# Routed expert network in a fused two-layer block: weight split beside the router, routing and slot scatters beside a shared expert on 512-token blocks

## The chip, the cores and the metric

The kernel runs on one core of a Trainium2 chip. The metric is the device time of one execution in microseconds. The engines named are TensorE (PE; its weight loads are PEld), VectorE (DVE), ScalarE (ACT), GpSimd (POOL) and SyncE (SP), which only issues transfers here.

## What is computed

The input is 16 x 256 tokens of width 256 (4096 tokens, 32 tiles of 128). Two layers follow each other, each an attention and a feed-forward part with a gated residual. The change lies in the feed-forward part of the first layer, a mixture of 8 routed experts (two per token) and one shared expert:

```python
def _mlp(x, w1, w2, w3):
    h = jax.nn.silu(x @ w1.T) * (x @ w3.T)
    return h @ w2.T
logits = xt @ gate_w.T
scores = jax.nn.softmax(logits.astype(jnp.float32), axis=-1)
biased = scores + gate_bias
_, indices = jax.lax.top_k(biased, TOPK)
weights = jnp.take_along_axis(original_scores, indices, axis=1)
...
for e in range(E):
    y = y + _mlp(xt, w1[e], w2[e], w3[e]) * combine[:, e:e + 1]
z = _mlp(xt, sw1, sw2, sw3)
return (y + z).reshape(shape)
...
x = x + jnp.tanh(g_ffn[0]) * _L0_ffn_ref(_layernorm(x, axis=-1), ...)
```

The inner width of an expert is 512.

## The kernel before

The whole program is a row of stages with a barrier between them: setup, attention of layer 0, the expert network (`moe`), attention of layer 1, and the last feed-forward part. Every fp32 product is made as three fp16 products (`three_products`): each operand is split into a high part (a ScalarE copy to fp16) and a low part (a subtraction, original minus high part).

`moe` is itself a row of stages, each a block of its own:

1. `load_split`, first on the router's weights ("wg"), then on the 27 expert matrices ("we", 512 KB each; 9 experts, three matrices each). SyncE loads into four staging buffers, ScalarE writes the high part, VectorE the low part. A buffer is loaded again when its low part is done.
2. `moe_router`, for each tile: VectorE normalises, ScalarE makes the high part, VectorE the low part (`row`, two buffers), SyncE stores the row to DRAM (`rows`, from which tokens are gathered later), TensorE transposes it and computes the 8 logits. `high` of tile t waits until the store of tile t-2 has landed, as the buffer is the same.
3. `moe_route`: some sixty small VectorE operations on all tiles at once (softmax, two picks of the best expert, counts by a TensorE product, running sums, the slot `POS` of each token, the table `ETAB` that gives the expert of each slot tile). TensorE, ScalarE and GpSimd have next to nothing to do in it.
4. `mlp_phase` with the tag "ms", the shared expert, tile by tile (128 tokens): gate and up products of 512 columns, SiLU and product, four fp32 transposes of the hidden values, split, down product of 256 columns. Beside it `slot_table` runs on GpSimd: 64 indirect transfers (32 tiles, two picks), each of which writes 128 token numbers of 4 bytes to their slots in DRAM. They go in 16 groups of 4. Before a group's index and value buffers `idx` and `val` are written again, GpSimd waits until the transfer that last read them has landed. When all have landed, SyncE reads the table back, TensorE transposes it, and VectorE writes `IDS`.
5. `mlp_phase` with the tag "me", the routed experts, on 72 slot tiles. Its gathers need `IDS`.

In the slot scatter these lines set the order:

```python
if not first:
    scattered[q].wait(pool, i, 0)
nc.gpsimd.tensor_copy(idx[q][:], POS[:, k, bass.ds(t, 1)]).then_inc(copied, 1)
nc.gpsimd.tensor_copy(val[q][:], tok[:, bass.ds(t, 1)]).then_inc(copied, 1)
```

## Time and profile before

| | us |
|---|---|
| median of 3 runs | 2516.06 (2513.68 to 2517.75) |
| profiled execution, its own time | 2506.78 |
| span of its trace | 2504.8 |
| TensorE busy in the span | 1948.7 (78%) |
| VectorE busy | 1609.6 (64%) |
| ScalarE busy | 1111.6 (44%) |
| GpSimd busy | 876.2 (35%) |

The profiled execution is one run of its own, 9.3 us below the median of the others. Times in the trace count from the start of the span. The busy share is a mean over stages with different limits; the stages of `moe` lie between 715 and 1410 us. A row's releaser, behind an arrow, is what ended the idle time before an instruction. TensorE's granted clock is given as a share of 2.4 GHz, so 0.50 is 1.2 GHz.

### The profile page before, as it was taken

The numbers are of one execution on the slowest core, as the hardware profiler recorded it, in microseconds if no ns is written. First come the engines' busy times: TensorE is split into PE (matmuls) and PEld (weight loads), VectorE is DVE, ScalarE is ACT, GpSimd is POOL, SyncE is SP. The second block draws the span as 40 slices with busy tenths as digits, with TensorE's granted clock in tenths as the row PEclk, the third lists the DMA queues.
The fourth block names the chain that finished last, engine by engine and source line by source line (L and its number), as shares of the span: only waits on it lengthen the run. The fifth ranks groups of instructions, "written<-read, shape, count | busy, mean of one in ns | idle before, by whom it ended". The sixth has DMA issues, their size and how long they took to land. (4 is left out here: it accounts for less than half of the span.)

```text
span 2504.8 us, 48924 instructions
## 1 busy us (share of the span) xinstructions
PE 1948.7 (78%) x14975; PEld 1386.5 (55%) x14984; DVE 1609.6 (64%) x3340; ACT 1111.6 (44%) x2557; POOL 876.2 (35%) x1363
## 2 busy tenths in 40 slices
PE   1798988988904597099999679898998889994275
PEld 1576676766603364066666456676666667673122
DVE  5777777877567543044444357777777777776797
ACT  1354444544434122022222146666666666673363
POOL 2000000000000243322332377777776777762004
PEclk9899999999955799599999899999999999997598
DMA  3000000000043000012221133223222232321001
GB/s 101 9 5 8 8 4 8 8 4 4 1 160 128 7 0 1 25 54 66 70 73 57 47 97 79 61 64 83 74 71 70 62 75 74 75 56 36 0 0 67
DMA packets 91507, 118.61 MB, mean 47 GB/s; under 512 B 18264, under 2 KB 60904, under 8 KB 91368
## 3 DMA queue, kind: packets, MB, share of 16 engines
q1 hardware_dynamic: 80872, 94.74, 13.8%
q0 software_dynamic: 8576, 17.87, 2.7%
q10 hardware_dynamic: 1920, 4.19, 0.5%
q8 instruction: 81, 1.33, 0.2%
q14 instruction: 58, 0.48, 0.1%
HBM read 56.92 MB, written 17.90 MB: 30 GB/s over the span
## 5 line engine op out<-in xcount | busy, mean ns | idle before, releaser
L1112 ACT ACTIVATE a_P<-a_pS,a_NM 128x256 f32<-128x256 f32 x512 | 237.2, 470 | 158.1 <-DVE a_NM L1212 157.8
L941 POOL TENSOR_SCALAR a_P<-a_P,a_RS 128x256 f32<-128x256 f32 x512 | 255.3, 499 | 113.2 <-DVE a_RS L1216 75.6
L504 PE MATMUL a_pT<-a_Q,a_K 128*128 128x256 f32 x1024 | 243.0, 383 | 8.6 <-ACT a_PT L587 8.6
L1212 DVE TENSOR_REDUCE a_NM<-a_pS 128x2 f32<-128x512 f32 x256 | 175.5, 686 | 96.6 <-PE a_pS L1027 95.0
L587 ACT ACTIVATE a_PT<-a_pT 128x512 f32<-128x512 f32 x256 | 151.2, 597 | 187.5 <-PE a_pT L504 187.1
L420 POOL TENSOR_TENSOR a_cl<-a_ctxin,a_ch 128x512 f16<-128x512 f32 x16 | 18.6, 1160 | 542.5 <-ACT a_ch L557 542.5
L504 PEld LDWEIGHTS a_pT<-a_Q,a_K 128*128 128x128 f32 x1024 | 183.6, 190 | 38.8 <-ACT a_PT L587 16.5
L1222 DVE TENSOR_TENSOR a_PL<-a_pT,a_PH 128x512 f16<-128x512 f32 x256 | 173.6, 678 | 48.2 <-ACT a_PH L1121 48.0
L1121 ACT ACTIVATE a_PH<-a_pT 128x512 f16<-128x512 f32 x256 | 153.1, 598 | 110.0 <-PE a_pT L1035 95.5
L1035 PE MATMUL a_pT<-g_ident,a_P 128*128 128x128 f32 x1024 | 157.9, 277 | 43.8 <-POOL a_P L941 34.8
L694 DVE TENSOR_REDUCE a_M<-a_pS 128x2 f32<-128x512 f32 x256 | 162.8, 682 | 32.8 <-PE a_pS L483 32.2
L1035 PEld LDWEIGHTS a_pT<-g_ident,a_P 128*128 128x128 f32 x1024 | 117.4, 141 | 74.9 <-POOL a_P L941 52.4
L1027 PE MATMUL a_pS<-a_KZ,a_QS 128*128 128x256 f16 x512 | 125.9, 273 | 0.0
L1026 PE MATMUL a_pS<-a_KD,a_QS 128*128 128x256 f16 x512 | 125.8, 273 | 0.0
L1707 ACT ACTIVATE me_hh<-me_pH 128x512 f16<-128x512 f32 x72 | 43.0, 597 | 175.7 <-PE me_pH L1692 175.7
L99 PE MATMUL a_pF<-a_ch,xw_XW 128*128 128x256 f16 x512 | 98.3, 276 | 27.2 <-DVE a_VL L1205 23.1
L1756 DVE TENSOR_TENSOR me_h<-me_SG,me_pU 128x512 f32<-128x512 f32 x72 | 49.5, 687 | 98.5 <-PE me_pU L99 98.5
L1705 ACT ACTIVATE me_SG<-me_pG 128x512 f32<-128x512 f32 x72 | 43.0, 597 | 147.8 <-PE me_pG L99 147.8
L99 PE MATMUL me_pG<-mo_w1h,me_xt 128*128 x288 | 98.7, 384 | 6.9 <-issue 6.9
L1112 ACT ACTIVATION_READ_ACCUMULATOR a_P<-a_pS,a_NM 128x1 f32 x512 | 102.8, 201 | 0.0
L99 PE MATMUL a_pF<-a_xh,xw_XW 128*128 128x256 f16 x512 | 98.9, 273 | 2.4 <-DVE a_k L1198 2.4
L1023 PE MATMUL a_pS<-a_maskq,g_identb 128*128 128x512 bf16 x256 | 97.4, 380 | 2.9 <-POOL a_maskq L931 2.4
(410 smaller groups left out, 5507.5 us busy)
## 6 DMA issues: line engine op xcount, KB each, us to landing
a_KD<-a_KN SPq DMA_DIRECT2D x128, 128.0 KB
a_QS<-a_QN SPq DMA_DIRECT2D x128, 128.0 KB
we_stage<-mw SPq DMA_DIRECT2D x24, 512.0 KB, 4.7
ys<-me_yb SPq DMA_DIRECT2D x72, 128.0 KB, 1.7
a_ctxin<-ctxT SPq DMA_DIRECT2D x32, 256.0 KB, 2.8
a_KZ<-a_KN SPq DMA_DIRECT2D x64, 128.0 KB
g_X<-x SPq DMA_DIRECT2D x1, 4096.0 KB, 15.0
rows<-mr_row SPq DMA_DIRECT2D x32, 128.0 KB, 1.7
```

Of the source, the lines that this page charges most:

```text
L99: last = nc.tensor.matmul(out, a(kt), b(kt), start=(n == 0), stop=(n == 3 * chunks - 1))
L504: last = nc.tensor.matmul(pT[h % 2][:, kt, :], K32[par][h % 2][:, h // 2, kt * P:(kt + 1) * P], Q32[par][:, h // 2, :], start=True, stop=True)
L587: nc.scalar.activation(PT[h % 8][:], pT[h % 2][:], ACT.Exp, scale=float(dh) ** -0.5).then_inc(p_ready.sem, 1)
L694: nc.vector.reduce_max(M[:, k % 2, k - k % 2:k - k % 2 + 2], pS[k % 2][:], AX.X).then_inc(s_max.sem, 1)
L941: last = nc.gpsimd.tensor_scalar(P32[u % 4][:, a, :], P32[u % 4][:, a, :], RS[u % 4][:, a:a + 1], LIFT, ALU.mult, ALU.mult)
L1026: nc.tensor.matmul(out[:, a, :], q, KD2[par][a][:, p2, :], start=False, stop=False)
L1027: last = nc.tensor.matmul(out[:, a, :], q, KZ[par][a][:, p2, :], start=False, stop=(a == 1))
L1035: last = nc.tensor.transpose(pT[u % 2][:, a, kt, :], P32[u % 4][:, a, kt * P:(kt + 1) * P], ident[:])
L1112: last = nc.scalar.activation(P32[u % 4][:, a, :], pS[u % 2][:, a, :], ACT.Exp, bias=NM[u % 4][:, a:a + 1], accum_out=SM[u % 4][:, a:a + 1])
L1121: nc.scalar.activation(PH[p2 % 2][:, :, :, j * P:(j + 1) * P].rearrange("p a k q -> p (a k) q"), pT[u % 2][:].rearrange("p a k q -> p (a k ...
L1212: nc.vector.tensor_reduce(NM[u % 4][:], pS[u % 2][:], AX.X, ALU.max, negate=True).then_inc(s_max.sem, 1)
L1222: nc.vector.tensor_tensor(PL[p2 % 2][:, :, :, j * P:(j + 1) * P].rearrange(f), pT[u % 2][:].rearrange(f), PH[p2 % 2][:, :, :, j * P:(j + 1 ...
```

## The change

- `load_split` for the router's and the experts' weights goes. The 27 loads, high parts and low parts move into the block of `moe_router`: SyncE issues the loads, ScalarE makes the high parts (`weight_high`, one a tile), GpSimd the low parts. The row stores move from SyncE to ScalarE. Loops are unrolled.
- `moe_route`, `slot_table` and the shared expert's `mlp_phase` become one block, `moe_shared`. The shared expert works on 8 blocks of 512 tokens. Its weights are the stationary operand of gate and up, so the hidden values come out transposed and the four transposes a tile go. One step g (32 in all) makes 128 of the 512 hidden rows for 512 tokens. Behind gate and up of steps 4, 8, ... stand the four down products of the block before (`down`), and those of the last block stand at the end. Gate and up have two PSUM buffers each; `h`, `SG`, `hh` and `hl` have one.
- The routing operations are put behind VectorE's `hidden` of steps 0 to 9 (`routing`). The slots are final in step 7 (`placed`).
- The 64 scatters read `POS` and `tok` directly and are issued one after the other, with one wait by SyncE at their end.
- The rotary tables are freed behind attention 0; that moves addresses only.

```diff
-def moe_router(nc, ctx, X, mean, rstd, XT, gwh, gwl, rows_d, L, consts):
+def moe_router(nc, ctx, X, mean, rstd, XT, gw_d, rows_d, L, consts, jobs):
     s = Scope(nc, ctx, "mr")
+    NS = 4
...
+    stage = [s.sb(f"stage{i}", [P, KD * F0]) for i in range(NS)]
...
+            sp.dma_start(gin[:], gw_d.rearrange("(k p) n -> p k n", p=P)).then_inc(gate_in, 16)
+            for j, (src, hi, lo) in enumerate(jobs):
+                if j >= NS:
+                    sp.wait_ge(w_lo, j - NS + 1)
+                sp.dma_start(stage[j % NS][:].rearrange("p (a b) -> p a b", a=src.shape[1]), src).then_inc(staged[j % NS], 16)
+        @block.gpsimd
+        def _(pool):
+            for j, (src, hi, lo) in enumerate(jobs):
+                pool.wait_ge(w_hi, j + 1)
+                nc.gpsimd.tensor_tensor(lo, stage[j % NS][:], hi, ALU.subtract).then_inc(w_lo, 1)
...
+            dve.wait_ge(gate_hi, 1)
+            nc.vector.tensor_tensor(gwl[:], gin[:], gwh[:], ALU.subtract).then_inc(gate_lo, 1)
...
+            def high(t):
                 xn_ready.wait(act, t, 1)
-                if pair is not None:
-                    stored[q].wait(act, pair, 0)
+                if t > 1:
+                    stored[t % 2].wait(act, t // 2, 0)
                     xt_full.wait(act, t, -1)
-                nc.scalar.activation(row[q][:, 0, :], xn[q][:], ACT.Copy).then_inc(hi_ready.sem, 1)
-            def logits(t, q):
+                nc.scalar.activation(row[t % 2][:, 0, :], xn[t % 2][:], ACT.Copy).then_inc(hi_ready.sem, 1)
+            def store(t):
+                lo_ready.wait(act, t, 1)
+                nc.scalar.dma_start(rows[t, :, :], row[t % 2][:].rearrange("p a d -> p (a d)")).then_inc(stored[t % 2].sem, 16)
+            def logits(t):
                 l_full.wait(act, t, 1)
-                nc.scalar.activation(L[:, bass.ds(t, 1), :].rearrange("p a e -> p (a e)"), pL[q][:], ACT.Copy).then_inc(l_out.sem, 1)
-            high(0, 0, None)
-            high(1, 1, None)
-            with act.Fori(0, TILES // 2 - 1) as i:
-                for q in range(2):
-                    high(i * 2 + 2 + q, q, i + 1)
-                    logits(i * 2 + q, q)
-            logits(TILES - 2, 0)
-            logits(TILES - 1, 1)
+                nc.scalar.activation(L[:, t, :], pL[t % 2][:], ACT.Copy).then_inc(l_out.sem, 1)
+            def weight_high(j):
+                src, hi, lo = jobs[j]
+                act.wait_ge(staged[j % NS], 16 * (j // NS + 1))
+                nc.scalar.activation(hi, stage[j % NS][:], ACT.Copy).then_inc(w_hi, 1)
+            high(0)
+            high(1)
+            for t in range(TILES):
+                store(t)
+                if t < len(jobs):
+                    weight_high(t)
+                if t + 2 < TILES:
+                    high(t + 2)
+                logits(t)
...
+def moe_shared(nc, ctx, X, XT, W1, W3, W2, consts, gb_d, slots_d, L, POS, GW, ETAB, IDS):
+    ident, gates = consts[0], consts[7]
+    s = Scope(nc, ctx, "ms")
     TE = [P, TILES, NE]
+    BLOCKS, BT = TILES // 4, 4 * P
+    STEPS = BLOCKS * FK
+    SG, h = s.sb("SG", [P, BT]), s.sb("h", [P, BT])
...
+    scan = (bi, cand)
...
+            sp.wait_ge(zero_ready, 1)
+            by_slot = slots_d.rearrange("(s p) a -> s (p a)", p=P)
+            sp.dma_start(by_slot, table[:]).then_inc(zeroed, 16)
+            sp.wait_ge(scattered, 16 * TOPK * TILES)
+            sp.dma_start(table[:], by_slot).then_inc(table_in, 16)
...
+            pool.wait_ge(zeroed, 16)
+            pool.wait_ge(placed, 1)
+            nc.gpsimd.nop(nofuse=True)
+            for t in range(TILES):
+                for k in range(TOPK):
+                    nc.gpsimd.indirect_dma_start(out=slots_d, out_offset=bass.IndirectOffsetOnAxis(ap=POS[:, k, t:t + 1], axis=0),
+                                                 in_=tok[:, t:t + 1], in_offset=None).then_inc(scattered, 16)
...
+            def up(g):
+                n, m = g // FK, g % FK
+                ts, fs = slice(n * BT, (n + 1) * BT), slice(m * P, (m + 1) * P)
+                for bank, W, full, free in ((pG, W1, gate_full, silu_ready), (pU, W3, up_full, h_ready)):
+                    if g > 1:
+                        free.wait(pe, g, -1)
+                    three_products(nc, bank[g % 2][:], lambda kt: W[0][:, NE, kt, fs], lambda kt: W[1][:, NE, kt, fs],
+                                   lambda kt: XT[:, 0, kt, ts], lambda kt: XT[:, 1, kt, ts], KD).then_inc(full.sem, 1)
+            def down(t):
+                j = t % 4
+                hl_ready.wait(pe, (t // 4 + 1) * FK, 0)
+                if t > 1:
+                    y_out.wait(pe, t, -1)
+                js = slice(j * P, (j + 1) * P)
+                three_products(nc, pY[t % 2][:], lambda k: hh[:, k, js], lambda k: hl[:, k, js],
+                               lambda k: W2[0][:, NE, k, :], lambda k: W2[1][:, NE, k, :], FK).then_inc(y_full.sem, 1)
+            for g in range(STEPS):
+                up(g)
+                if g == COUNT_AT:
+                    pe.wait_ge(counts_in, 1)
+                    nc.tensor.matmul(pC[:, 0:256], earlier[:], picked[:].rearrange("p t e -> p (t e)"), start=True, stop=True)
+                    nc.tensor.matmul(pC[:, 256:512], ones[:], picked[:].rearrange("p t e -> p (t e)"), start=True, stop=True)\
+                        .then_inc(counted, 1)
+                if g % FK == 0 and g:
+                    for t in range(g - 4, g):
+                        down(t)
+            for t in range(TILES - 4, TILES):
+                down(t)
+            pe.wait_ge(table_in, 16)
+            nc.tensor.transpose(pI[:], table[:], ident[0:SLOT_TILES, 0:SLOT_TILES]).then_inc(ids_full, 1)
...
+            def silu(g):
+                gate_full.wait(act, g, 1)
+                if g:
+                    h_ready.wait(act, g, 0)
+                nc.scalar.activation(SG[:], pG[g % 2][:], ACT.Silu).then_inc(silu_ready.sem, 1)
+            def high(g):
+                n, m = g // FK, g % FK
+                h_ready.wait(act, g, 1)
+                if n:
+                    y_full.wait(act, 4 * n, 0)
+                nc.scalar.activation(hh[:, m, :], h[:], ACT.Copy).then_inc(hh_ready.sem, 1)
+            for g in range(STEPS):
+                silu(g)
+                high(g)
...
+            def routing(g):
+                if g == 0:
+                    softmax_out()
+                    choose(0)
+                elif g == 1:
+                    choose(1)
+                elif g == COUNT_AT:
+                    counts()
+                elif g == COUNT_AT + 1:
+                    running(0)
+                elif g == COUNT_AT + 2:
+                    running(1)
+                elif g == COUNT_AT + 3:
+                    expert_starts()
+                elif g == COUNT_AT + 4:
+                    positions()
+                elif g == COUNT_AT + 6:
+                    expert_table()
+            def hidden(g):
+                up_full.wait(dve, g, 1)
+                silu_ready.wait(dve, g, 1)
+                if g:
+                    hh_ready.wait(dve, g, 0)
+                    hl_ready.wait(dve, g, 0)
+                V.tensor_tensor(h[:], SG[:], pU[g % 2][:], ALU.mult).then_inc(h_ready.sem, 1)
+            def low(g):
+                n, m = g // FK, g % FK
+                hh_ready.wait(dve, g, 1)
+                if n:
+                    y_full.wait(dve, 4 * n, 0)
+                V.tensor_tensor(hl[:, m, :], h[:], hh[:, m, :], ALU.subtract).then_inc(hl_ready.sem, 1)
+            def result(t):
+                y_full.wait(dve, t, 1)
+                V.scalar_tensor_tensor(X[:, t, :], pY[t % 2][:], gates[:, 2:3], X[:, t, :], ALU.mult, ALU.add).then_inc(y_out.sem, 1)
+            softmax_in()
+            for g in range(STEPS):
+                hidden(g)
+                routing(g)
+                if g >= FK and g % FK == 0:
+                    for t in range(g - 4, g):
+                        result(t)
+                low(g)
+            for t in range(TILES - 4, TILES):
+                result(t)
+            y_out.wait(dve, TILES, 0)
+            dve.wait_ge(ids_full, 1)
+            V.tensor_copy(IDS[:], pI[:])
...
+    jobs = [(w_d[n][e].rearrange("(k p) n -> p k n", p=P), W[n][0][:, e, :, :].rearrange(flat), W[n][1][:, e, :, :].rearrange(flat))
+            for e in (NE, *range(NE)) for n in ("w1", "w3", "w2")]
...
-        load_split(nc, c2, "wg", [(gw_d.rearrange("(k p) n -> p k n", p=P), gw[0][:].rearrange(flat), gw[1][:].rearrange(flat))], KD * NE)
+        moe_router(nc, c2, X, mean, rstd, XT, gw_d, rows_d, L, consts, jobs)
     with ExitStack() as c2:
-        jobs = [(w_d[n][e].rearrange("(k p) n -> p k n", p=P), W[n][0][:, e, :, :].rearrange(flat), W[n][1][:, e, :, :].rearrange(flat))
-                for n in ("w1", "w3", "w2") for e in range(NE + 1)]
-        load_split(nc, c2, "we", jobs, KD * F0)
+        moe_shared(nc, c2, X, XT, W["w1"], W["w3"], W["w2"], consts, gb_d, slots_d, L, POS, GW, ETAB, IDS)
     with ExitStack() as c2:
-        moe_router(nc, c2, X, mean, rstd, XT, gw[0], gw[1], rows_d, L, consts)
-    with ExitStack() as c2:
-        moe_route(nc, c2, L, gb_d, consts[7], consts, tok, POS, GW, ETAB)
-    with ExitStack() as c2:
-        table = slot_table(nc, c2, slots_d, tok, POS, IDS, consts[0])
-        mlp_phase(nc, c2, "ms", TILES, X, XT, W["w1"], W["w3"], W["w2"], consts, None, table)
-    with ExitStack() as c2:
-        mlp_phase(nc, c2, "me", SLOT_TILES, X, XT, W["w1"], W["w3"], W["w2"], consts, (IDS, ETAB, rows_d, y_d), None, (XW, next_w_d))
+        mlp_phase(nc, c2, "me", SLOT_TILES, W["w1"], W["w3"], W["w2"], consts, (IDS, ETAB, rows_d, y_d), (XW, next_w_d))
```

ScalarE in the router's block. `mr_row` is the row's high part, `mo_L` the logits, `mo_w1h` and the like are high parts of expert weights. Before, the split and then the router's loop body:

```order
L273 ACTIVATE mo_w1h<-we_stage 128x1024 x9
L273 ACTIVATE mo_w3h<-we_stage 128x1024 x9
L273 ACTIVATE mo_w2h<-we_stage 128x1024 x9
L260 UNCONDITIONAL_BRANCH
L1303 UNCONDITIONAL_BRANCH
L1310 ACTIVATE mr_row<-mr_xn 128x256 x2
```

Now, from the start of the router's block:

```order
L1320 ACTIVATE mr_row<-mr_xn 128x256 x2
L1324 DMA rows<-mr_row 128x512
L1333 ACTIVATE mo_w1h<-mr_stage 128x1024
L1320 ACTIVATE mr_row<-mr_xn 128x256
L1328 ACTIVATE mo_L<-mr_pL 128x8
L1324 DMA rows<-mr_row 128x512
L1333 ACTIVATE mo_w3h<-mr_stage 128x1024
```

The row store and one weight's high part now stand between two rows' high parts, in ScalarE's own queue.

GpSimd at the slot scatter (`slots` is the table in DRAM). Before, one group of the loop:

```order
L1522 COPY st_idx<-g_POS 128x1
L1523 COPY st_val<-mo_tok 128x1
L1522 ISA
L1522 COPY st_idx<-g_POS 128x1
L1523 COPY st_val<-mo_tok 128x1
L1524 ISA
L1527 DMA slots<-st_val,st_idx 9216x1 x4
```

Now:

```order
L1431 MEMSET ms_earlier 128x128
L1432 MEMSET ms_ones 128x128
L1434 AFFINE_SELECT ms_earlier<-ms_earlier 128x128
L1437 MEMSET ms_table 72x128
L1443 DMA slots<-ms_tok,g_POS 9216x1 x64
```

The copies, and with them the waits for landed transfers, are gone, and all 64 transfers stand in a row.

VectorE in step 7 of the shared expert's block, now (`ms_h` is the hidden product, `ms_hl` its low part; before, the routing rows stood in a block of their own, ahead of all `ms_h` rows):

```order
L1618 TENSOR_TENSOR ms_h<-ms_SG,ms_pU 128x512
L1575 TENSOR_TENSOR ms_excl<-ms_excl,ms_bi 128x256
L1576 TENSOR_TENSOR ms_excl<-ms_excl,ms_tot 128x256
L1577 TENSOR_TENSOR ms_excl<-ms_excl,ms_first 128x256
L1579 TENSOR_TENSOR ms_tmp<-ms_oh,ms_excl 128x256
L1580 TENSOR_REDUCE ms_posf<-ms_tmp 128x32
L1579 TENSOR_TENSOR ms_tmp<-ms_oh,ms_excl 128x256
L1580 TENSOR_REDUCE ms_posf<-ms_tmp 128x32
L1581 CAST g_POS<-ms_posf 128x64
L1625 TENSOR_TENSOR ms_hl<-ms_h,ms_hh 128x512
```

The slots are ready only when VectorE has passed seven steps of the shared expert.

## Rows read from the trace of the kernel before

**Rows 1.** Windows by stage: busy time and count per engine, PEclk, DMA share, GB/s
```profile
717.50:769.50 52.00, 0.00 (x0) 0.00 (x0) 33.07 (x27) 28.52 (x27) 0.00 (x0) 0.50 0.82 272
769.50:818.30 48.80, 30.07 (x320) 25.00 (x320) 34.90 (x96) 17.90 (x64) 0.00 (x0) 0.50 0.26 86
818.30:845.30 27.00, 0.61 (x2) 0.13 (x2) 20.83 (x63) 1.70 (x2) 1.62 (x7) 0.50 0.00 0
845.30:990.00 144.70, 141.42 (x896) 89.33 (x896) 59.57 (x96) 39.49 (x65) 60.15 (x145) 0.98 0.01 1
990.00:1055.00 65.00, 0.38 (x1) 0.18 (x1) 0.23 (x1) 0.00 (x0) 20.79 (x49) 0.52 0.01 1
```

**Rows 2.** Timeline, 1038 to 1060 us: start, length, engine, line, operation
```profile
1041.44 0.95 POOL L1527 DMA_INDIRECT slots<-st_val,st_idx  x1 [0.30 <-issue]
1042.70 0.96 POOL L1527 DMA_INDIRECT slots<-st_val,st_idx  x1 [0.31 <-issue]
1049.77 0.30 SPq L1509 DMA_DIRECT2D st_back<-slots  x1
...
1055.37 0.18 POOL L1609 COPY me_idx<-mo_IDS 128x1 uint32<-128x1 uint32 x1 [11.71 <-POOLq L1600]
```

**Rows 3.** Timeline of SyncE, 715 to 819 us
```profile
715.15 0.38 SPq L266 DMA_DIRECT2D wg_stage<-gate_w  x1
...
818.40 0.34 SPq L1387 DMA_DIRECT2D rt_gb<-gate_bias  x1
```

**Rows 4.** Page, part 6: DMA issues, size, median us to landing
```profile
we_stage<-mw SPq DMA_DIRECT2D x24, 512.0 KB, 4.7
...
rows<-mr_row SPq DMA_DIRECT2D x32, 128.0 KB, 1.7
```

**Rows 5.** Groups of instructions, 700 to 1056 us, with mean ns of one
```profile
L1760 DVE TENSOR_TENSOR ms_hl<-ms_pH,ms_hh 128x512 f16<-128x512 f32 x32 | 22.1, 691 | 15.9 <-ACT ms_hh L1707 15.7
L1756 DVE TENSOR_TENSOR ms_h<-ms_SG,ms_pU 128x512 f32<-128x512 f32 x32 | 22.0, 687 | 45.5 <-PE ms_pU L99 44.3 <-issue 1.3
...
L1707 ACT ACTIVATE ms_hh<-ms_pH 128x512 f16<-128x512 f32 x32 | 19.1, 597 | 78.2 <-PE ms_pH L1692 78.2
L1705 ACT ACTIVATE ms_SG<-ms_pG 128x512 f32<-128x512 f32 x32 | 19.1, 597 | 23.6 <-PE ms_pG L99 23.6
...
L1310 ACT ACTIVATE mr_row<-mr_xn 128x256 f16<-128x256 f32 x32 | 13.2, 416 | 21.9 <-DMA rows<-mr_row 17.3 <-DVE mr_xn L1278 4.6
...
L273 ACT ACTIVATE mo_w1h<-we_stage 128x1024 f16<-128x1024 f32 x9 | 9.5, 1056 | 9.3 <-DMA we_stage<-mw 9.1 <-DMA we_stage<-msw 0.3
```

**Rows 6.** Tile me_stage: duration ns min/median/max of the GpSimd subtraction
```profile
L1606 POOL TENSOR_TENSOR xw_XW<-me_stage,xw_XW x8: 2124/2126/2132, 1109.1 to 1373.1; 128x1024 f16<-128x1024 f32 x8
```

**Rows 7.** Timeline of TensorE, one tile of the shared expert
```profile
903.65 0.38 PE L99 MATMUL ms_pG<-mo_w1h,xw_XW 128*128 128x512 f16 x1
...
906.24 0.27 PE L99 MATMUL ms_pY<-mo_w2h,ms_hh 128*128 128x256 f16 x1
...
907.55 0.60 PE L1692 MATMUL ms_pH<-g_ident,ms_h 128*128 128x128 f32 x4
```

**Rows 8.** Timeline of VectorE: the slot positions
```profile
842.74 0.19 DVE L1482 CAST g_POS<-rt_posf 128x64 uint32<-128x64 f32 x1
```

**Rows 9.** Timeline of GpSimd, index copies of three of the groups
```profile
860.43 0.18 POOL L1522 COPY st_idx<-g_POS 128x1 uint32 x1 [5.80 <-DMA slots<-st_val,st_idx]
...
865.30 0.18 POOL L1522 COPY st_idx<-g_POS 128x1 uint32 x1
...
1008.89 0.18 POOL L1522 COPY st_idx<-g_POS 128x1 uint32 x1 [1.88 <-DMA slots<-st_val,st_idx]
...
1017.12 0.18 POOL L1522 COPY st_idx<-g_POS 128x1 uint32 x1 [1.95 <-DMA slots<-st_val,st_idx]
...
1033.85 0.18 POOL L1522 COPY st_idx<-g_POS 128x1 uint32 x1 [0.90 <-DMA slots<-st_val,st_idx]
...
1037.83 0.18 POOL L1522 COPY st_idx<-g_POS 128x1 uint32 x1 [2.17 <-DMA slots<-st_val,st_idx]
```

323 lines of the change are left out of this document (133 added, 190 removed).

## The prediction

> **What bounds the kernel now.** I read the busy time by stage first, then the timeline where the stages meet, then the groups inside each. The expert network is a row of stages with a barrier between, so a microsecond saved in one is a microsecond saved in the whole as long as its slowest chain is what gets shorter. Four stages lie before the routed experts [rows 1]. The weight split (717.5 to 769.5) keeps the transfer engines 0.82 busy at 272 GB/s and TensorE idle. The router (769.5 to 818.3) moves 86 GB/s; its ScalarE waits for landed row stores (17.3 us of waits behind 13.2 us of work, [rows 5]). The routing (818.3 to 845.3) is VectorE alone. The shared expert fills TensorE until 990 (141.4 of 144.7 us), but the routed experts cannot start then: from 990 to 1055 TensorE has one product, and only GpSimd works. The last slot scatter is issued at 1042.70, its landing releases SyncE's read of the table at 1049.77, and the next stage starts at 1055.37 [rows 2]. So the scatters, not TensorE, end the shared expert's stage. From the first load at 715.15 [rows 3] to 1055.4 it is 340 us. The routed experts behind are not touched, and I carry them over unchanged.
>
> **Router and split in one block.** Removed is the split's own time, 52 us, with the router weights' block of 2.4 us ahead of it. What is added to the router is, for each of 27 tiles, a high part of 1.06 us on ScalarE [rows 5], a subtraction on GpSimd, which takes 2.13 us for the same shape in the routed stage [rows 6], and a 512 KB load. The sums by engine are all below the 100.8 us that the two stages take: GpSimd 27 x 2.13 = 57 us; ScalarE 27 x (1.06 + 0.42 + 0.15, the logits copy from 17.9 - 13.2 us over 32) = 44 us and 32 issues.
>
> The chain is what counts. ScalarE now issues the store of tile t, makes a weight's high part, and then waits until that same store has landed, since the next row's high part of tile t+2 goes to the same buffer. Before, SyncE issued the stores, and two were under way together. Now ScalarE cannot issue store t+1 until store t has landed. A tile takes at least 1.7 us to landing [rows 4] + 0.42 + 0.15 + about 0.2 for hand-overs = 2.45 us; the weight's high part is hidden in the landing. Beside it 655 KB move per tile, which at 272 GB/s is 2.4 us: the transfer engines are nearly as tight, so a store shares them with a load. The landing grows with the queue (a load lands after 4.7 us where several are under way, [rows 4]). I take 0.3 us more, 2.75 us a tile. The bounds are 2.45 and 3.3 us (a GpSimd subtraction of 2.13 and the two VectorE operations of 0.42 in turn, plus hand-overs). The stage: 4 us for the router weights, 27 x 2.75, 5 x 2.45 for the tiles without weights, 3 us for the end = 93.5 us, against 103.2 now. The gain is 10 us (from 18 less to 5 more time), far below the 52 us of the stage removed. The block ends at 808.6.
>
> The Trainium skill (SBUF — State Buffer, the part on the shared port pair) says that a GpSimd operation and a VectorE operation with two SBUF inputs lock each other out for a whole instruction; by it the upper bound of 3.3 us a tile would be the value. No row before has the two side by side in this form.
>
> **The shared expert and the routing.** Now a tile costs TensorE 2.59 us for gate and up (903.65 to 906.24), 1.31 us for down (to 907.55) and the transposes behind [rows 7]. The transposes go; 32 steps of 2.59 and 32 downs of 1.31 are 125 us. The routing's 24.6 us (818.3 until the slots' cast ends at 842.93, [rows 1, 8]) now lies between the shared expert's own operations on VectorE. Up to step 7 these add 8 hidden products and 7 low parts of 0.69 [rows 5] = 10.4 us, four results (2 us), and one wait for four down products (5.2 us) with hand-overs to ScalarE's 0.6 us copies: about 6 us. The slots are ready 43 us into the block, not 24.6. TensorE starves meanwhile: `h` has one buffer, and gate and up may run only two steps ahead. Step 7's low part releases the downs of block 1, done at about 50 us; that includes 1 us for a start at 1.2 GHz (clock 0.50 in the stages before, 0.98 in this one, [rows 1]). Behind it stand 23 x 2.59 + 24 x 1.31 = 91 us, then 4 us for the last block's SiLU, product, copy and subtraction in a row before the last downs: 145 us, and 2.5 us to the next stage. In the steady part VectorE needs 4 x 1.38 + 2 = 7.5 us a block of four tiles and TensorE 15.6, so nothing else waits.
>
> **The scatters** decide. Two things are removed: 128 small copies and the wait for landing between groups. GpSimd's issue takes 1.26 us apiece (1041.44 to 1042.70, [rows 2]): 64 are 81 us. But are landings as fast as issues? Within a group the four are issued 1.26 us apart, and the copies for the second and the fourth, each released by the landing of the transfer before, should stand 2.5 us apart. They stand 4.87 us apart in the loop's first group, 3.98 in its last, 8.23 in the slowest [rows 9]; over all 15 groups of the loop the mean is 4.11 us. So four scatters under way land every 2.06 us. This is a rate, not only a delay: if each had the same delay, the landings would keep the distance of the issues. I take 2.06 us. Then the last lands 1 + 64 x 2.06 + 3 us behind the slots: 43 + 136 = 179 us. From the read of the table to the next stage it is 5.6 us [rows 2]. The stage takes 184.5 us and ends at 993, and TensorE has an idle gap of some 35 us in front of that, down from 65.
>
> The Trainium skill (DMA: Bandwidth & Descriptors, "Anatomy of one DMA") puts most of a transfer's fixed 2 us in the receipt of its last write, which queued transfers overlap; by it the scatters would go at the pace of issue. The spacing of the landings [rows 9] does not agree with it for these 4-byte writes. The same page's table of specifications says that transfers under 512 bytes are read-modify-writes, which speaks for the slower rate.
>
> **The sum.** The routed experts start at 993 instead of 1055.4: 62 us less. The profiled execution of 2506.8 us would be 2445; it lies 9 us below the median of the runs shown, so for a median I forecast 2516 - 62 = 2454 us.
>
> **Rivals.**
> - *Issue-paced scatters* (0.30). Landings overlap as issues do: 43 + 1 + 81 + 5 + 5.6 = 136 us, less than TensorE's 147.5, which then ends the stage, at 956. That is 99 us less: 2417. For it: the short distances (some groups have two landings released almost together). Against: the mean of 2.06.
> - *Slower landings under a deep queue* (0.17). Now the queue empties after each four; with 64 queued it never does. A whole group takes 12.3 us (865.30 to 1037.83 is 14 groups, [rows 9]), of which some 11 us are from first issue to last landing, 2.75 us apiece: 44 + 176 + 3 + 5.6 = 229 us, end at 1037, 18 us less: 2498.
> - *The landings lose more than the waits cost* (0.05; slower than before). With the rest as forecast, the start at 1055.4 is reached when each scatter takes (1055.4 - 808.6 - 52.6) / 64 = 3.03 us. At the slowest group's 8.23 / 2 = 4.1 us the stage lasts 315 us, 68 us over: 2584. For it: one group has it. Against: only one in fifteen.
> - *The router's block is slower than forecast* (0.06), 3.3 us a tile, with the scatters as in my case: 47 us less, 2469.
> - The split into two states, issue-paced or landing-paced, is the main doubt; my own case has 0.40. Its own range is 2440 to 2475 (1.8 to 2.4 us a scatter, router's block 88 to 100 us). Within 0.2% of before, about what a measurement of this kernel can tell from no change, lies only a narrow band around 3.03 us a scatter: 0.02.
>
> **Range and chances.** From the issue-paced case with the shorter router block (2417 - 8) to nearly the deep-queue case: 2405 to 2495. Faster 0.93, same 0.02, slower 0.05.
>
> **What the changed profile would show.** The router's block 88 to 100 us long, with ScalarE idle before each row's high part for the landed store, and GpSimd's subtractions near 2.13 us. VectorE's cast of the slots 43 us into the shared block. GpSimd's 64 scatters 1.26 us apart in one row of 81 us (if they stand further apart, their queue is full). SyncE's read of the table 179 us into the block; if it stands at 130 us or before TensorE's last product, the landings overlap and the first rival is right. TensorE near 2.59 us a step from step 9 on. A low clock in the first 45 us of the block, where TensorE has gaps, would move the TensorE end later, but counts only in the issue-paced case. What would make me wrong is above all the landing rate, 64 times in the sum: 0.1 us in it is 6.4 us.

## The result, and the profile after

The changed kernel took 2429.93 us (median of 4 runs, 2424.18 to 2436.15) beside 2516.9 us of the kernel before: ratio 0.9654, 95% interval 0.9626 to 0.9683. That is 24 us less than the 2454 forecast and inside the range. Timed again, in two later batches of runs (both on one chip; on which the first ran is not recorded), the same program took 2504.67 us (7 runs, 2491.85 to 2509.36) and 2501.20 us (7 runs, 2496.73 to 2509.09), both times 0.9945 of the kernel before (0.9922 to 0.9969, and 0.9927 to 0.9964). So it is faster in all three, but by 3.5% once and by 0.55% twice. The first part of this section reads the profile of the fast measurement (2431.72 us); the experiments are mostly about the difference.

Windows of the changed kernel, cut at its stages, against [rows 1]: length, busy time and count of each engine, PEclk, DMA share, GB/s.

```profile
713.30:818.40 105.10, 24.10 (x320) 21.09 (x320) 51.45 (x97) 43.69 (x92) 58.06 (x27) 0.50 0.59 175
818.40:862.30 43.90, 34.52 (x160) 16.40 (x161) 30.84 (x78) 12.67 (x20) 1.81 (x8) 0.85 0.01 2
862.30:966.00 103.70, 98.71 (x604) 60.02 (x603) 48.41 (x81) 27.56 (x47) 63.01 (x64) 0.97 0.03 2
```

The first row is the joined block of weights and router: 105 us, no shorter than the two stages that it replaces (100.8 us in [rows 1]), although it does both at once. From its first load to the load of the bias it is 106.4 us (713.36 to 819.74, below), where it was 103.2 before. The second runs until the scatters start, the third while they are issued, with TensorE busy in 98.71 of 103.7 us.

The router's rows and (last line) normalised tiles in that block, by tile: durations min/median/max, first and last start, what ended the idle time before it, and the landing of its store. Line 1324 answers to the last of [rows 4], line 1320 to the mr_row line of [rows 5].

```profile
L1320 ACT ACTIVATE mr_row<-mr_xn x32: 416/416/417, 715.8 to 815.4; 128x256 f16<-128x256 f32 x32
...
L1324 ACTq DMA_DIRECT2D rows<-mr_row x32: 326/326/392, 716.7 to 817.1; - x32
...
  DMA rows<-mr_row: 53.3, 29
...
DMA to landing us min/median/max: 1.7/3.2/5.7
...
L1290 DVE TENSOR_SCALAR mr_xn<-g_X,g_mean,g_rstd x32: 398/406/2280, 715.4 to 812.2; 128x256 f32<-128x256 f32 x32
```

Beside the weight loads a store lands after 3.2 us, up to 5.7, where it was 1.7; ScalarE sits idle for it 53.3 us. VectorE's normalisation takes 0.40 us at its shortest and 2.28 us at its longest, where a GpSimd subtraction lies beside it. The low part of a row, which reads two tiles, is held up likewise; here from 743.22 to 745.02 us, beside a subtraction that ends at 744.74:

```profile
742.51 2.23 POOL L1280 TENSOR_TENSOR mo_w3l<-mr_stage,mo_w3h 128x1024 f16<-128x1024 f32 x1 [0.69 <-ACT mo_w3h L1333]
...
743.22 1.80 DVE L1294 TENSOR_TENSOR mr_row<-mr_xn,mr_row 128x256 f16<-128x256 f32 x1 [0.46 <-ACT mr_row L1320]
```

The timeline of the shared block and what frames it: SyncE's three transfers, then VectorE's cast of the slot positions, then GpSimd's first and last scatter and the first index copy of the next stage. They answer to [rows 2, 3, 8].

```profile
713.36 0.38 SPq L1270 DMA_DIRECT2D mr_gin<-gate_w  x1
...
819.74 0.34 SPq L1418 DMA_DIRECT2D ms_gb<-gate_bias  x1
...
951.09 0.29 SPq L1423 DMA_DIRECT2D ms_table<-slots  x1
...
861.22 0.20 DVE L1581 CAST g_POS<-ms_posf 128x64 uint32<-128x64 f32 x1
...
862.30 1.23 POOL L1443 DMA_INDIRECT slots<-ms_tok,g_POS  x1 [40.99 <-DVE g_POS L1581]
...
943.56 0.95 POOL L1443 DMA_INDIRECT slots<-ms_tok,g_POS  x1 [0.30 <-issue]
968.20 0.19 POOL L1708 COPY me_idx<-mo_IDS 128x1 uint32<-128x1 uint32 x1 [23.69 <-POOLq L1415]
```

The positions of the slots are cast at 861.2, 41.5 us into the block. The 64 scatters leave from 862.30 to 943.56, 1.29 us apart. The table is read at 951.09, only 7.5 us after the last of them was issued: landings keep up with issues. TensorE's last product of the block starts at 966.85 and the routed experts' first index copy follows at 968.20, against 1055.37 in [rows 2]: 87.2 us earlier. The medians differ by 87.0 us, but the two profiled executions by 75.1 only: some of the 87.2 us is given back behind this point. The view of the gathers of the second attention (first and last start) shows most of it:

```profile
L901 POOL DMA_INDIRECT a_routed<-ys,a_pick x64: 971/1049/1084, 1331.7 to 2107.1; - x64
```

The first starts 87.1 us earlier than in the profile of before (1418.8 there) and the last 78.1 earlier (2185.2 there): 9 us lost in a stage that the diff does not touch. In the middle of the scatters TensorE is never idle for long:

```profile
880.00:940.00 60.00, 59.52 (x370) 36.11 (x371) 26.94 (x45) 16.52 (x28) 45.67 (x48) 1.00 0.03 2
```

One line in this profile looks harmless. Two rows of ScalarE's timeline, each a copy that opens a block of four tiles and so waits for TensorE's four down products of the block before:

```profile
916.81 0.63 ACT L1497 ACTIVATE ms_hh<-ms_h 128x512 f16<-128x512 f32 x1 [6.00 <-PE ms_pY L99]
...
936.62 0.63 ACT L1497 ACTIVATE ms_hh<-ms_h 128x512 f16<-128x512 f32 x1 [10.21 <-remote]
```

`remote` stands where a signal arrived but no instruction whose end fits it is in the records. The wait is 6.00 us in the two blocks before and 10.21 us here, 4.2 us more. In the two later measurements of this program the longest wait with this mark is some 31 us, and the experts start 63 to 71 us later.

### The profile page after: what moved, and what is told of

It reads as the page before. It is cut to its first block and busy times, and to the rows that moved or that the text cites. A ratio compares the mean times of both kernels' runs of the same rounds, so it can differ in the third digit from the quotient of the medians.

```text
span 2430.0 us, 47541 instructions
## 1 busy us (share of the span) xinstructions
PE 1941.7 (80%) x14847; PEld 1372.2 (56%) x14856; DVE 1592.0 (66%) x3313; ACT 1108.4 (46%) x2557; POOL 917.0 (38%) x1262
## 5 line engine op out<-in xcount | busy, mean ns | idle before, releaser
L99 PE MATMUL me_pU<-mo_w3h,me_xt 128*128 x288 | 98.3, 382 | 0.0
```

Of the source, the lines that this page charges most:

```text
L99: last = nc.tensor.matmul(out, a(kt), b(kt), start=(n == 0), stop=(n == 3 * chunks - 1))
```

## The experiments

The runs came in four batches, each on one chip with its own runs of the kernel before: 2522.62 us (19 runs) for the first four kernels, 2515.48 (10) for the next four, 2515.27 (7) for three, 2518.53 (10) for the last. The first, second and third batch ran on three different chips, the last on that of the second.

### The scatters alone

The kernel before, with its scatters freed of the copies and of the waits between groups:

```diff
-        def scatter(i, first):
...
-        scatter(0, True)
-        with pool.Fori(1, TILES * TOPK // NB) as i:
-            scatter(i, False)
+        for t in range(TILES):
+            for k in range(TOPK):
+                nc.gpsimd.indirect_dma_start(out=slots_d, out_offset=bass.IndirectOffsetOnAxis(ap=POS[:, k, t:t + 1], axis=0),
+                                             in_=tok[:, t:t + 1], in_offset=None).then_inc(all_scattered, 16)
```

> The kernel before, with only the slot scatters issued one after the other without waits (the rest is as before: split, router, routing and shared expert in their own stages). Theory A, landings overlap as issues do: the scatters end 81 + 8 us behind their start, before TensorE's last product at 990, the routed experts start at 992 instead of 1055, about 63 us less (ratio 0.975). Theory B, landings come every 2 us once several are under way: the scatters end 847 + 135 = 982 and the gain is the same; theory C, at 2.75 us: end at 1028, gain 25 us. The read of the table by SyncE tells A (near 936) from B (near 982).

Measured: 2520.62 us, 0.9992 (0.9981 to 1.0004): nothing gained. The scatters did go at the pace of issue, 850.8 to 930.6 us, and the table was read at 939.5. But the routed experts started at 1069.7, later than before. A window of 60 us in the middle of the scatters:

```profile
870.00:930.00 60.00, 7.85 (x28) 3.95 (x28) 1.86 (x3) 0.60 (x1) 45.64 (x48) 0.53 0.02 0
```

and three rows of the view of waits, 830 to 1000 us: who waited for what, us in total, times, longest:

```profile
ACT ms_hh L1691 <- remote: 51.2, 2, 45.7
...
PE ms_pY L99 <- issue: 38.1, 2, 36.2
...
DVE g_X L1728 <- remote: 31.6, 2, 28.9
```

TensorE worked 7.85 of the 60 us. So landings are not the limit that the prediction took them for; something else happens to TensorE, ScalarE and VectorE while scatters leave closely, and it eats the whole gain.

### Scatters in fours, each four landed

The changed kernel, with a wait for everything issued before each four scatters:

```diff
             for t in range(TILES):
+                if t and t % 2 == 0:
+                    pool.wait_ge(scattered, 16 * TOPK * t)
                 for k in range(TOPK):
```

> The changed kernel, with GpSimd waiting for all landings after every four scatters, as the kernel before does in effect; nothing else is changed. If the waits were the cost: a group takes about 11 us again, 16 groups 180 us, the table is read at 862 + 180 = 1042 instead of 951, and the time is 75 to 95 us above the changed kernel (2510). If the small index copies were a large part of the cost before, the groups take under 9 us and the time is less than 50 us above.

Measured: 2530.95 us, 1.0033 (1.0018 to 1.0047). GpSimd waited 115.8 us in 15 waits, the scatters lasted from 867.4 to 1059.6, and the experts started at 1071.8. TensorE was busy 59.41 of 60 us between 880 and 940, and then waited 100.8 us for the table. A group took 12.6 us, more than the 11 expected, and the read of the table stood at 1067.4, not 1042. With this wait left in, the whole change is worth nothing.

### Four row buffers in the router's block

```diff
-    xn = [s.sb(f"xn{i}", [P, D]) for i in range(2)]
-    row = [s.sb(f"row{i}", [P, 2, D], F16) for i in range(2)]
+    NR = 4
+    xn = [s.sb(f"xn{i}", [P, D]) for i in range(NR)]
+    row = [s.sb(f"row{i}", [P, 2, D], F16) for i in range(NR)]
...
-                if t > 1:
-                    stored[t % 2].wait(act, t // 2, 0)
+                if t >= NR:
+                    stored[t % NR].wait(act, t // NR, 0)
```

> The changed kernel with four buffers instead of two for the normalised rows and their fp16 parts in the router's block, so that ScalarE waits for the landing of the store of two tiles further back. Theory A, the landing of the store is the chain (53 us of ScalarE's waits): a tile takes about 2.5 us instead of 3.45, set by the loads, the block 80 to 88 us instead of 105, 17 to 25 us less (2408). Theory B, GpSimd's and VectorE's locking each other out is the chain: less than 5 us.

Measured: 2472.80 us, 0.9810 (0.9783 to 0.9837). SyncE's timeline, the frame of the block:

```profile
716.52 0.38 SPq L1271 DMA_DIRECT2D mr_gin<-gate_w  x1
...
796.26 0.34 SPq L1419 DMA_DIRECT2D ms_gb<-gate_bias  x1
```

and the view of the rows' tile, for VectorE's low part and the landing of the stores:

```profile
L1295 DVE TENSOR_TENSOR mr_row<-mr_xn,mr_row x32: 410/412/2142, 719.6 to 792.3; 128x256 f16<-128x256 f32 x32
...
DMA to landing us min/median/max: 1.7/3.8/6.0
```

From the gate's load to the bias's it is 79.7 us instead of 106.4 (713.36 to 819.74). (In the other three profiles of this block with two row buffers it is 98.0, 108.0 and 108.0 us; in all with four, 79.5 to 81.3.) The stores land no sooner (3.8 us median) and VectorE is still stretched (2142 ns at the longest), so what bounded the block was ScalarE's wait for the buffer that a store still reads. Yet the routed experts started at 1014.5, where some 945 was to be had (148.5 us behind the bias load, as in the first profile of the changed kernel). The 60 us after 860, as a window:

```profile
860.00:920.00 60.00, 11.19 (x36) 4.77 (x36) 2.83 (x4) 2.45 (x4) 45.55 (x48) 0.50 0.02 1
```

and five operations from the timeline of the same stretch, of TensorE, ScalarE, VectorE, ScalarE and TensorE:

```profile
869.14 0.63 PE L99 MATMUL ms_pU<-xw_XW,mo_w3l 128*128 128x512 f16 x1
...
880.40 0.60 ACT L1491 ACTIVATE ms_SG<-ms_pG 128x512 f32<-128x512 f32 x1 [12.75 <-issue]
...
897.20 0.69 DVE L1619 TENSOR_TENSOR ms_h<-ms_SG,ms_pU 128x512 f32<-128x512 f32 x1 [28.76 <-remote]
...
897.92 0.63 ACT L1498 ACTIVATE ms_hh<-ms_h 128x512 f16<-128x512 f32 x1 [16.92 <-issue]
...
899.33 0.40 PE L99 MATMUL ms_pY<-mo_w2h,ms_hh 128*128 128x256 f16 x1 [29.55 <-issue]
```

These rows show the stall from near. The product `h` needs TensorE's up-product, whose last matmul starts at 869.14, and ScalarE's SiLU, done at 881.0. VectorE starts it at 897.20, 16 us after the later of the two. ScalarE's copy of it follows within 0.03 us, and TensorE's next product 0.06 us behind VectorE's low part (898.58 to 899.27). So instructions on ScalarE and VectorE start at once behind each other, but those that wait for a TensorE result (`gate_full`, `up_full`, `y_full`) wait some 15 to 30 us; and since `h` and the banks have one and two buffers, everything stands. The clock falls to 0.50 as well (the lower of its two levels, 1.2 GHz), with TensorE idle for most of the window; in the windows with no stall it is 1.00.

These waits have to be read with care. The 64 scatters give 1024 landing signals (16 each). Counted up to the read of the table, the trace of the kernel before holds 1011 of them and the first profile of the changed kernel 910, but this one 164. Of the engines' own signals it holds 5 between 860 and 920 us, where the first profile has 112 between 880 and 940. So `remote` and `issue` often stand here only because the signal is missing from the records; the starts and lengths of the instructions don't depend on that.

### Router and weights apart again

The changed kernel's shared block behind the old two stages:

```diff
-def moe_router(nc, ctx, X, mean, rstd, XT, gw_d, rows_d, L, consts, jobs):
+def moe_router(nc, ctx, X, mean, rstd, XT, gwh, gwl, rows_d, L, consts):
...
+        load_split(nc, c2, "we", jobs, KD * F0)
+        moe_router(nc, c2, X, mean, rstd, XT, gw[0], gw[1], rows_d, L, consts)
```

> The changed kernel with the weight split and the router of the kernel before, each a stage of its own again; the shared expert's block as changed. Theory A, the fusion of split and router gives nothing, since ScalarE waits for each row store to land (105 us for the block against 103 us for the two stages): within 3 us of the changed kernel, rather 2 us faster. Theory B, the fusion gives something that the block's length does not show (a warmer clock later on): more than 5 us slower.

Measured: 2489.25 us, 0.9870 (0.9850 to 0.9891), 59 us above the changed kernel's first measurement. The bias was loaded at 817.72, 104.8 us behind the first load, within the 98.0 to 108.0 us of the joined block: joining gained no time that stands clear of this spread. TensorE was starved here too (10.38 of 60 us from 880 to 940), and the experts started at 1035.9. That is where the changed kernel starts them when it stalls (1031.6 and 1039.2, below), and yet it takes 2501 to 2505 us then. The gathers of the second attention, by tile:

```profile
L901 POOL DMA_INDIRECT a_routed<-ys,a_pick x64: 971/1049/1083, 1397.8 to 2167.2; - x64
```

From first to last they take 769.4 us here, 766.4 in the kernel before and 767.0 in the one with the scatters alone. In every kernel with the joined block they take 773.9 to 777.4 us. So this second attention takes 4.5 to 8 us longer behind the joined block than in this run. Its loops are also unrolled where the old stages have loops, and these runs do not show which of the two it is, or why.

At this point three of three kernels with free scatters stalled and the changed kernel had not. Either its program was spared or its measurement; the next four runs were to tell.

### The changed kernel again, beside four in flight

First a wait that keeps scatters apart, with four row buffers:

```diff
             for t in range(TILES):
+                if t > 1:
+                    pool.wait_ge(landed[t % 2], 16 * TOPK * (t // 2))
                 for k in range(TOPK):
```

> The changed kernel with four row buffers in the router block, and before each group of four scatters (from the third on) a wait until the group two before it has landed, so that at most eight are in flight. Theory Q (the run of the four row buffers lost its gain because the ungated scatters delay what the other engines wait for; eight in flight is what the kernel before had, without any such delay): TensorE is busy over 90% of the time while the scatters are issued, as it was in the kernel before, the index copy of the routed experts starts at 945 to 970 us instead of 1014.5, and the time is 2405 to 2435 us against 2522 of the kernel before (0.954 to 0.965). Theory R (the delay has nothing to do with how many are in flight, but with this chip or with where the program lies in memory): the same starvation as with ungated scatters, index copy near 1014, 2473 us (0.981).

A group here is two scatters, so at most four were in flight, not eight as the expectation says; the kernel before also had four.

> The changed kernel with four row buffers and ungated scatters once more, beside the changed kernel itself. Theory Q, and theory R by placement of the program: as before, about 2473 us with TensorE idle for most of 80 us. Theory R by chip: the same on a chip where the changed kernel itself stalls, and about 2410 us on one where it doesn't.

> The changed kernel itself, unaltered, on the chip of the other runs of this call. If the stall of the three ungated variants comes from the chip, it is here too: TensorE starved for 60 to 80 us behind the first scatter, 2485 us or so against 2522 (0.985). If it comes from the kernels and not the chip: TensorE busy over 90% as in its first profile, 0.9654 again, 2435 us.

> The changed kernel with four row buffers, ungated, but each of the 64 scatters writes only the tokens of partitions 0 to 63 (half of the slots keep token 0, so the routed experts work on wrong rows; the amount of their work is unchanged). If the delay grows with the number of 4-byte writes under way, it is halved or gone: index copy at 945 to 985 us and 2405 to 2445 us. If it comes with the number of scatter instructions or with something else, index copy near 1014 and 2473 us.

```diff
-out_offset=bass.IndirectOffsetOnAxis(ap=POS[:, k, t:t + 1], axis=0), in_=tok[:, t:t + 1]
+out_offset=bass.IndirectOffsetOnAxis(ap=POS[0:64, k, t:t + 1], axis=0), in_=tok[0:64, t:t + 1]
```

Measured: four in flight 2447.11 us, 0.9729 (0.9708 to 0.9749); the ungated four-row kernel 2476.55 (one run); the changed kernel 2504.67, 0.9945; half of the writes 2476.11 (one run). A window of 60 us beside the scatters, with four in flight:

```profile
860.00:920.00 60.00, 60.00 (x365) 35.39 (x363) 28.93 (x47) 18.99 (x32) 27.60 (x29) 1.00 0.02 1
```

of the ungated four-row kernel:

```profile
860.00:920.00 60.00, 5.52 (x24) 3.36 (x24) 2.07 (x3) 1.75 (x3) 43.34 (x46) 0.54 0.02 0
```

of the changed kernel:

```profile
880.00:940.00 60.00, 11.25 (x36) 4.82 (x36) 4.23 (x8) 3.05 (x5) 45.68 (x48) 0.51 0.02 1
```

and of the one with half of the writes, 50 us, since its scatters end sooner:

```profile
860.00:910.00 50.00, 8.22 (x18) 2.21 (x18) 5.07 (x10) 1.86 (x3) 37.41 (x42) 0.52 0.02 1
```

The changed kernel itself stalls: 11.25 of 60 us, where its first profile has 59.52. The view of its waits between 864 and 960 us, for VectorE and TensorE:

```profile
DVE ms_h L1618 <- remote: 62.5, 3, 31.5
...
PE ms_pY L99 <- issue: 29.6, 4, 24.6
PE ms_pY L99 <- DVE g_X L1629: 27.7, 1, 27.7
```

Its experts started at 1039.2, not 968.2, and that is the difference between the two measurements: 71 us later, 74.7 us more time. So the stall comes with the change itself and not only with its variants, and the first measurement is the one that was spared. In this batch four row buffers are worth 28.1 us (2504.67 less 2476.55, the latter a single run). With four in flight no stall is left, and the scatters take 838.7 to 973.8 us, 2.14 us apart; TensorE then waits 42.8 us for the table. The experts start at 985.1, later than the 945 to 970 expected of eight in flight. With half as many 4-byte writes in each scatter the stall is the same (8.22 of 50 us), so halving the writes does not ease it. It does bring the last landing forward: the table is read 2.8 us behind the last issue (916.24 less 913.42), where it is 6.8 to 9.0 us with all writes. With landings so early some two or three scatters can be in flight there, if the others land as the last does (an estimate, 2.8 us at 1.21 us apart); that is no more than in the run with at most four, which does not stall. (That kernel leaves the token of half of the slots at 0; the amount of the experts' work is unchanged.)

### Paced by time, and six in flight

The wait of the last kernel keeps fewer scatters in flight and also spreads them. Pacing without any wait for a landing:

```diff
                                                  in_=tok[:, t:t + 1], in_offset=None).then_inc(scattered, 16)
+                    for r in range(2):
+                        if t + k + r:
+                            pool.wait_ge(paused, 2 * (TOPK * t + k) + r)
+                        nc.gpsimd.memset(pause[:], 0.0).then_inc(paused, 1)
```

> The changed kernel with four row buffers and ungated scatters, but with two small GpSimd memsets behind each scatter, so that the scatters leave about every 2.1 to 2.4 us and GpSimd never waits for a landing (eight_in_flight above had in truth four in flight, since a group there is two scatters, and a pitch of 2.1 us). Theory P (what delays TensorE's signals is how densely the scatters are issued): no stall, TensorE busy over 90% until about 942 us, the last scatter at 975 to 990, the index copy at 990 to 1000, 2450 to 2462 us against 2515 to 2522 of the kernel before. Theory F (it is the wait for landings that protects): TensorE stalls as in the ungated runs, with waits put down to remote of 15 us and more, and since the scatters last longer the index copy comes after 1040, over 2495 us.

Six in flight, by the wait for the third group back:

```diff
             for t in range(TILES):
+                if t > 2:
+                    pool.wait_ge(landed[(t - 3) % 4], 16 * TOPK * ((t - 3) // 4 + 1))
                 for k in range(TOPK):
```

> As the gated run with four row buffers, but with up to six scatters in flight (groups of two, a wait for the third group before). A landing there took about four pitches, 8.4 us, so six in flight allow a pitch of 1.4 us. If the delay of the other engines grows smoothly with the density of scatters: waits of 5 to 10 us begin to show at TensorE, the index copy starts at 955 to 985 and the time is 2415 to 2445 us. If there is a threshold between a pitch of 1.4 and 1.26: no stall, index copy at 945 to 952, 2405 to 2412 us, 0.956 of the kernel before. If the threshold lies under six in flight: starved as ungated, index copy near 1014, 2473 us.

> The ungated kernel with four row buffers, as the reference of this call: on the two chips so far 2473 and 2477 us with the index copy at 1014.5 and 1011.0. About the same is expected wherever scatters at a pitch of 1.26 us starve the other engines; 2405 to 2415 us would mean a chip or a placement on which they don't, as in the first profile of the changed kernel.

Measured: paced 2454.25 us (one run); six in flight 2426.94 us (2421.34 to 2438.19), 0.9643 (0.9627 to 0.9659); ungated 2472.23 (one run). The same 60 us, paced:

```profile
860.00:920.00 60.00, 60.00 (x364) 35.40 (x363) 28.84 (x46) 18.96 (x32) 54.05 (x82) 1.00 0.02 1
```

six in flight:

```profile
860.00:920.00 60.00, 39.33 (x220) 22.40 (x218) 15.98 (x26) 9.79 (x17) 37.91 (x40) 0.89 0.03 1
```

ungated:

```profile
860.00:920.00 60.00, 10.25 (x35) 4.41 (x32) 3.44 (x5) 2.45 (x4) 45.67 (x48) 0.50 0.02 1
```

The scatters by tile (durations, first and last start), paced:

```profile
L1445 POOL DMA_INDIRECT slots<-ms_tok,g_POS x64: 963/966/1524, 837.5 to 978.5; - x64
```

and six in flight:

```profile
L1448 POOL DMA_INDIRECT slots<-ms_tok,g_POS x64: 953/960/1477, 839.9 to 946.6; - x64
```

The stall goes with the distance between scatters, with four row buffers throughout:

| kernel | distance, us | TensorE busy, of 60 us | experts start | time, us |
|---|---|---|---|---|
| paced, no wait | 2.24 | 60.00 | 988.6 | 2454.25 |
| four in flight | 2.14 | 60.00 | 985.1 | 2447.11 |
| six in flight | 1.69 | 39.33 | 976.1 | 2426.94 |
| ungated (three profiles) | 1.27 | 11.19, 5.52, 10.25 | 1014.5, 1011.0, 1013.8 | 2472.80, 2476.55, 2472.23 |

(The distance is last start less first over 63.) In the paced kernel GpSimd is busy 54.05 of 60 us and nothing stalls, so it is not GpSimd's being busy. The numbers with six in flight are those expected of a stall that grows smoothly with density. Six in flight is the best of these: it pays some stall, and the table comes before TensorE has done. Its profiled run was its slowest (2438.19 us); the other three are at 2421.34 to 2428.82.

### The changed kernel a third time

> The changed kernel itself a third time. It has been timed twice: 2429.93 us (0.9654 of the kernel before), with TensorE hardly delayed beside the scatters, and 2504.67 us (0.9945), starved for some 80 us behind them. If the first was an exception (one chip or one placement) and starvation at a pitch of 1.26 us is the rule, as in the six other profiles with ungated scatters: 2490 to 2510 us, index copy at 1030 to 1045. If it goes by chip with no rule: either of the two levels, about 2430 or about 2500, and all runs of one call at the same level. If it goes by single executions: both levels among the runs of this call.

Measured: 2501.20 us, 0.9945, all seven runs between 2496.73 and 2509.09; the experts started at 1031.6. The earlier repeat had been on this same chip, so this confirms the level but adds no chip. The levels did not mix within a batch. Eight profiles with scatters 1.21 to 1.28 us apart, on three chips and in five different programs, show the starvation; the first profile of the changed kernel is the only one without.

## Why the prediction was right, and where it was not

**The direction and the number.** Faster, with 2429.93 in the range of 2405 to 2495, came true in the first measurement. In the repeats the time lay 6 to 10 us above the range. That the first number came within 24 us is in part luck: the shared stage took 36 us less than forecast (148.5 against 184.5), the router's block 12.9 more, and 12.1 us of the profiled gain were given back behind the experts' start, where the prediction carried everything over unchanged. In the repeats a further cost was there, which no term stood for.

**Router and weights, forecast 93.5 us: mis-sized.** From first load to bias load, as the forecast counts, it measured 106.4 us, and 108.0 and 98.0 in the repeats. Only the last lies in the 88 to 100 us named; all lie below the 108.4 that 3.3 us a tile would give. The mechanism was as forecast (ScalarE idle for the landed store, 53.3 us), but a tile took (807.2 - 717.6) / 26 = 3.45 us, first to last high part of a weight, against 2.75 and even against the bound of 3.3. The failed number is "I take 0.3 us more": the store landed 1.5 us later at the median beside a load, and up to 4 us later. Four buffers took 26.6 us off, so the term was this wait and not the turns of GpSimd and VectorE. The turns are there, though: VectorE's low part, with its two SBUF inputs, stretched from 0.41 to 1.80 us beside GpSimd's subtraction of some 2.15. On this the trace agrees with the Trainium skill (SBUF — State Buffer, on the shared port pair). The normalisation, with one tile as input, stretched too, from 0.40 to 2.28 us. The bound of 3.3 us a tile, worked out from such turns, was passed since a store alone took 3.2 us to land at the median and 5.7 at most.

**Slots ready after 43 us: right** (41.5). **TensorE done after 145 us: right**, 147.2 us (819.74 to 966.96) with one small delay in it.

**The scatters, 2.06 us apiece: wrong, and this is the step that failed.** The sentence "This is a rate, not only a delay: if each had the same delay, the landings would keep the distance of the issues" was drawn from landings in groups of four with a pause behind each. Their distances (4.11 us at the mean for two issued 2.5 us apart) tell how delays differ within such a group, not how fast landings can follow each other. With all freed the table could be read 7.5 us after the last issue, in the first profile of the changed kernel, and after 6.8 to 9.0 us in the other ungated ones with all writes (951.8 less 945.0; 928.6 less 919.6). In the kernel before it was 7.1 us (1049.77 less 1042.70), paced 6.1, with four in flight 7.2, with six 7.3: about the same delay at every distance from 1.27 to 2.24 us, so a delay that overlaps and not a rate. The first rival (issue-paced, 0.30) was right: it gave 136 us to the next stage by the scatters, 147.5 by TensorE, against 148.5 measured (819.7 to 968.2). The Trainium skill (DMA: Bandwidth & Descriptors, "Anatomy of one DMA") puts most of a transfer's fixed time in the receipt of its last write; the prediction concluded from it that queued transfers overlap this time and then set that aside, and the runs bear the conclusion out for these 4-byte writes. The rival's 2417 us and the router's 12.9 us above forecast make 2429.9; 2429.93 was measured. That this fits so closely is chance, since 12.1 us behind the experts' start are in no term and the profiled run of before lies 9.3 us under its median.

**What no case had: the stall.** At a distance of 1.27 us TensorE stood for most of 80 us in eight of nine profiles. It takes back 63 to 71 us of the 87 that the change had won by the start of the experts in its first profile. The deep-queue rival (0.17) feared the right situation, a queue that never empties, but expected the landings to suffer; they did not, the other engines did. The profile of before could not show it: its scatters came four to 12.3 us [rows 9], and TensorE was busy 141.42 of 144.7 us beside them [rows 1]. The prediction put the scatters' effect on the other engines at nothing, without a reason.

**What stays open.** Which part of the chip holds the signals of TensorE back is not shown. Halving the 4-byte writes does not ease it, and it is not GpSimd's time (90% busy, no stall). How many scatters are in flight and how far apart they leave moved together in the other runs; the run with half the writes speaks for the distance, by the estimate above, but no run sets the two apart cleanly. It is also not shown whether the matmul itself ends late or only its signal, since the ends of matmuls are modelled. Nor is it shown whether the recording has a part in the stall. The stalled traces hold 150 to 164 of the 1024 landing signals, the one with six in flight 616, and those without a stall 869 to 1011 (910 in the first profile), so the records thin out with the stall, and every run on record has a recorded span and clock. A timing with nothing recorded would tell. And why the first measurement was spared is open: same program, same distance (1.29 us), hardly a stall. It may be the chip, which is not recorded; of the three chips known, all stalled, but the changed kernel itself ran on one of them only. Open too is why the second attention takes 4.5 to 8 us longer behind the joined block.

## What to carry to other kernels

When a stream of small indirect transfers is moved beside other engines' work, count not only when it ends but what it does to them: look for gaps, put down to `remote` or `issue`, on engines that have nothing to do with the stream, and try it with a bound on how many are in flight. Here a wait for the third pair back (six in flight) gave 2426.94 us where the free stream gave 2472.23, and four row buffers in place of two, for a store that lands late, gave 28 us. And distances read off instructions that stand behind waits for landings belong to that loop; they are no limit for the transfers. A time taken once, on one chip, can also be the exception: here the first measurement was.

## What the runs showed of the hardware that was not expected

- Indirect scatters of 128 four-byte writes land at the pace of their issue, one per 1.27 us; the last is followed by the dependent read after 6.8 to 9.0 us, and after 2.8 us with 64 writes in place of 128.
- While they leave 1.27 us apart, ScalarE and VectorE go on from TensorE's results 15 to 30 us late in eight of nine profiles (28.76, 29.45 and 31.5 us idle before single VectorE operations); at 1.69 us apart TensorE works 39.33 of 60 us, at 2.14 us and more all of it.
- The same program on the same data had this stall in two measurements and almost none in one, 2501 to 2505 us against 2430.
- A 128 KB store lands after 1.7 us at the median with no loads beside it, after 2.6 to 3.9 us at the median (up to 7.5) beside 512 KB loads.
